# A linear-attention recurrence: products of k and v written into the SBUF state buffer and scanned there, two channel chunks per instruction

## The chip, the cores and the metric

The kernel runs on one core of a Trainium2 chip. A core has five engines that run their own instruction streams and meet at semaphores: TensorE (PE, matrix products into PSUM; PEld in the profile is its loading of weights), VectorE (DVE), ScalarE (ACT), GpSimd (POOL) and SyncE (SP, which issues DMAs). SBUF and PSUM are the two on-chip memories, both with 128 partitions. The metric is the device time of one execution in microseconds, median of the runs. All data are fp32.

## What is computed

Sixteen sequences of 256 tokens by 512 channels pass through an encoder-decoder block (self attention, cross attention, MLP) and then an RWKV-like block. The change is in the recurrence of the second block. Cut to what matters, with H = 32 heads of S = 16 channels:

```
w = exp(-exp(time_decay + tanh(xw @ decay_w1) @ decay_w2)).reshape(B, L, H, S)
r, k, v = ((x_ @ W_.T).reshape(B, L, H, S) for x_, W_ in (...))
s0 = state[:, i0 + 2:i0 + 2 + S].reshape(B, H, S, S)

def step(s, inp):
    k_l, v_l, w_l, r_l = inp
    a = k_l[..., :, None] * v_l[..., None, :]
    out = jnp.einsum('bhs,bhst->bht', r_l, faaaa * a + s)
    return (a + w_l[..., None] * s, out)
_, outs = jax.lax.scan(step, s0, seq)        # over the 256 tokens
```

So for each channel (head, s) and each of the 16 value columns t of its head there is a first-order recurrence over the tokens: state(l+1) = w(l) state(l) + k(l) v(l). The output reads the state before it is updated, times r, summed over s. A group norm, a gate, an output product and a channel-mixing part follow.

## The kernel before

The program has four phases, one after the other: self attention (tiles s_), cross attention (x_), MLP (b_), and phase_c with the second block (c_). Only phase_c is touched. It starts about 2420 us into the span and takes the last 1830.

**Layout.** Channels lie on partitions: 512 channels are 4 chunks (KC = 4) of 128, tokens (T = 256) run along the free dimension. A tile is 128 x 4 x 256. `pair(x, i)` is chunks 2i and 2i+1, thus 128x512.

**Stages.** `phase_c` is a software pipeline written out by hand: `body(k, parts, par)` works, in one iteration, on the recurrence of sequence k ("wkv"), on what follows it for sequence k - 1 ("back": group norm, gate, Wo, channel mixing) and on what comes before it for sequence k + 1 and k + 2 ("front", "norm"). 14 iterations (k = 1 to 14) hold both wkv and back; k = 0 has no back, k = 15 no front. Each iteration has RS = 16 steps n, one for each value column. The table FILLS says which PSUM units (mw0, k0, o0, ...) TensorE fills at step n ahead of and behind the second half step; VectorE or ScalarE empties them. Each engine runs the same loop over n in its own order, so that table is the order of all four.

**The recurrence.** At step n:

- PE, `broadcast_v` (L1645): for each half step i = 0, 1, one matmul spreads column n of v over the 16 channels of its head, into `vb` in PSUM, chunks 2i and 2i+1. It waits until VectorE is done with what step n - 1 left there.
- DVE, `recur` (L1474, L1479): multiplies vb by kT in place in PSUM, then runs one TENSOR_TENSOR_SCAN for each of the two chunks, from wT (SBUF) and vb (PSUM), starting at s0, into `S[:, n % 4, c, 1:257]` in SBUF. S has four buffers, one for each of four steps in turn.
- ACT, `start_state` (L1355): copies s0 into column 0 of the S buffer.
- POOL (L1201): after both half steps and the start state, multiplies all four chunks of S by rT in place (128x1024). Called z here.
- PE, `sum_states` (L1656): at odd steps, sums z of an earlier pair of steps over the channels of each head into `acc`. With this the S buffers are free again (semaphore summed).

**Other work of the same engines in an iteration.** VectorE reads PSUM units (L1423 for the five mixes mw, mk, mr, mv, mg; L1430 r; L1436 and L1437 v; L1445 o; L1453 kv; L1427 g), takes norm statistics (L1405 to L1412) and the group norm's (L1489, L1493 to L1502). GpSimd has, besides z, five adds of 128x1024 after the five mixes (`add_xa`, L1159), the group norm (L1164 to L1173), the gate product zT times g2T (L1181, step 3), the inverse deviation (L1152, L1154), the shifted difference and the two sums of the channel mixing (L1186 at step 8, L1191 at steps 9 and 10), and L1194, L1212, L1216 at steps 15, 12 and 13. Each stands in POOL's queue right behind z of its step. The two channel-mixing sums release TensorE's product with fWk (unit kk0, step 11).

## Time and profile before

| | |
|---|---|
| median of 3 runs | 4260.67 us (4258.37 to 4265.11) |
| the profiled execution | 4252.74 us, span 4250.9 us |
| busy in the span | PE 88%, DVE 71%, ACT 48%, POOL 41% |
| one iteration of phase_c with all parts | about 105.5 us |
| busy in one such iteration (us) | PE 98.7, DVE 84.4, POOL 65.1, ACT 32.9 |

The profile is one execution on the core, read by a hardware profiler. Busy time of PE is modelled and includes overlap of a matmul with the next one, so 98.7 of 105.5 us is an order that is almost gapless, not a peak rate. A time in brackets behind a row is how long the engine was idle before it, and what released it. What one iteration costs is set stretch by stretch by the engine that has no idle time there.

### The profile page before, as it was taken

The numbers are of one execution on the slowest core, as the hardware profiler recorded it, in microseconds if no ns is written. First come the engines' busy times: TensorE is split into PE (matmuls) and PEld (weight loads), VectorE is DVE, ScalarE is ACT, GpSimd is POOL, SyncE is SP. The second block draws the span as 40 slices with busy tenths as digits, with TensorE's granted clock in tenths as the row PEclk, the third lists the DMA queues.
The fourth block names the chain that finished last, engine by engine and source line by source line (L and its number), as shares of the span: only waits on it lengthen the run. The fifth ranks groups of instructions, "written<-read, shape, count | busy, mean of one in ns | idle before, by whom it ended". The sixth has DMA issues, their size and how long they took to land. (4 is left out here: it accounts for less than half of the span.)

```text
span 4250.9 us, 71399 instructions
## 1 busy us (share of the span) xinstructions
PE 3730.4 (88%) x21636; PEld 2882.3 (68%) x21636; DVE 2998.0 (71%) x6732; ACT 2057.8 (48%) x5384; POOL 1742.2 (41%) x1210
## 2 busy tenths in 40 slices
PE   5998998588888886999999778999999999999976
PEld 4777777477777774899999655666666666666643
DVE  5777777477777775556556338888888878888872
ACT  4777777367777675545545322333333333333322
POOL 2444444144444441000000135666666666666652
PEclk9999999799999997999999889999999999999988
DMA  3434434344444443010010210000000000000000
GB/s 110 104 99 109 104 99 104 96 116 118 104 114 110 122 104 116 30 44 30 30 41 33 73 50 18 24 24 23 24 23 24 23 24 23 24 23 23 23 18 15
DMA packets 146611, 256.58 MB, mean 60 GB/s; under 512 B 27184, under 2 KB 32048, under 8 KB 145424
## 3 DMA queue, kind: packets, MB, share of 16 engines
q1 hardware_dynamic: 146448, 254.49, 22.0%
q8 instruction: 92, 1.51, 0.2%
q14 instruction: 71, 0.58, 0.0%
HBM read 107.62 MB, written 33.55 MB: 33 GB/s over the span
## 5 line engine op out<-in xcount | busy, mean ns | idle before, releaser
L1201 POOL TENSOR_TENSOR c_S<-c_S,c_rT 128x1024 f32<-128x1024 f32 x256 | 558.1, 2180 | 458.4 <-DVE c_S L1479 417.6
L1479 DVE TENSOR_TENSOR_SCAN c_S<-c_wT,c_s,c_vb 128x256 f32<-128x256 f32 x1024 | 709.0, 734 | 45.0 <-issue 2.7
L1474 DVE TENSOR_TENSOR c_vb<-c_kT,c_vb 128x512 f32<-128x512 f32 x512 | 352.4, 688 | 286.4 <-PE c_vb L1645 255.6
L348 POOL TENSOR_TENSOR x_prob<-x_prob,x_rsums 128x512 f32<-128x512 f32 x256 | 275.2, 1075 | 477.7 <-DVE x_rsums L510 477.7
L348 POOL TENSOR_TENSOR s_prob<-s_prob,s_rsums 128x512 f32<-128x512 f32 x256 | 275.2, 1075 | 431.0 <-DVE s_rsums L510 431.0
L1645 PE MATMUL c_vb<-c_vhl,c_spread 128*128 128x512 f32 x512 | 300.4, 597 | 73.6 <-DVE c_S L1479 60.6
L404 ACT ACTIVATE x_prob<-x_t,x_tmin 128x256 f32<-128x256 f32 x512 | 256.4, 502 | 218.3 <-DVE x_tmin L503 218.0
L404 ACT ACTIVATE s_prob<-s_t,s_tmin 128x256 f32<-128x256 f32 x512 | 256.5, 502 | 193.9 <-DVE s_tmin L503 193.6
L862 PE MATMUL b_ps<-b_ln_high,b_w_high 128*128 128x256 f32 x1024 | 290.9, 284 | 14.8 <-DVE b_ln_low L804 14.8
L863 PE MATMUL b_ps<-b_ln_low,b_w_high 128*128 128x256 f32 x1024 | 290.8, 284 | 0.0
L864 PE MATMUL b_ps<-b_ln_high,b_w_low 128*128 128x256 f32 x1024 | 290.8, 284 | 0.0
L499 DVE SCALAR_TENSOR_TENSOR x_ps_s<-x_ps_s,x_mask 128x512 f32<-128x512 f32 x256 | 177.8, 695 | 93.7 <-PE x_ps_s L592 72.9
L499 DVE SCALAR_TENSOR_TENSOR s_ps_s<-s_ps_s,s_mask 128x512 f32<-128x512 f32 x256 | 177.6, 694 | 90.3 <-PE s_ps_s L592 62.7
L1159 POOL TENSOR_TENSOR c_xmix<-c_xmix,c_xaT 128x1024 f32<-128x1024 f32 x80 | 174.1, 2176 | 145.8 <-DVE c_xmix L1423 135.1
L602 PE MATMUL x_ps_t<-w_ident,x_prob 128*128 128x128 f32 x1024 | 163.3, 283 | 71.8 <-ACT x_probT L414 62.6
L760 ACT ACTIVATE b_shared<-b_ps,w_cols 128x256 f32<-128x256 f32 x256 | 123.3, 481 | 206.8 <-PE b_ps L864 204.9
L503 DVE CUSTOM_DVE_ANT_0 x_t<-x_ps_s,x_mneg 128x256 f32<-128x256 f32 x512 | 197.1, 422 | 31.0 <-issue 3.3
L503 DVE CUSTOM_DVE_ANT_0 s_t<-s_ps_s,s_mneg 128x256 f32<-128x256 f32 x512 | 197.1, 422 | 29.3
L602 PE MATMUL s_ps_t<-w_ident,s_prob 128*128 128x128 f32 x1024 | 161.8, 281 | 59.7 <-ACT s_probT L414 51.0
L862 PEld LDWEIGHTS b_ps<-b_ln_high,b_w_high 128*128 128x128 f32 x1024 | 197.7, 193 | 15.8 <-ACT b_ln_high L748 15.2
L862 PE MATMUL b_ps<-b_w_high,b_act_high 128*128 128x512 f32 x512 | 201.6, 394 | 5.1 <-DVE b_act_low L825 5.0
L863 PE MATMUL b_ps<-b_w_low,b_act_high 128*128 128x512 f32 x512 | 199.5, 390 | 0.0
(266 smaller groups left out, 10572.4 us busy)
## 6 DMA issues: line engine op xcount, KB each, us to landing
s_stack<-s_parts_qk SPq DMA_DIRECT2D x384, 128.0 KB, 2.4
x_stack<-x_parts_qk SPq DMA_DIRECT2D x384, 128.0 KB, 2.4
s_x_in<-in_x SPq DMA_DIRECT2D x16, 512.0 KB, 3.6
s_xb<-in_x SPq DMA_DIRECT2D x16, 512.0 KB, 4.1
x<-s_x_out SPq DMA_DIRECT2D x16, 512.0 KB, 4.8
x_enc<-in_ctx SPq DMA_DIRECT2D x16, 512.0 KB, 4.4
x_x_in<-x SPq DMA_DIRECT2D x16, 512.0 KB, 3.7
x_xb<-x SPq DMA_DIRECT2D x16, 512.0 KB, 4.1
```

Source lines behind the costliest of these rows:

```text
L348: nc.gpsimd.tensor_tensor(prob[:, h % 4, :, :], prob[:, h % 4, :, :], rsums[:, h, :].unsqueeze(2).to_broadcast([P, TC, T]), ALU.mult).then ...
L404: op = nc.scalar.activation(prob[:, n % 4, tc, :], t[:, n % 2, tc, :], ACT.Exp, bias=tmin[:, n, tc:tc + 1], scale=-1.0, accum_out=psums[:, ...
L499: nc.vector.scalar_tensor_tensor(ps_s[:, n % 2, :, :], ps_s[:, n % 2, :, :], -SCALE, mask[:, :, :], ALU.mult, ALU.mult)
L503: op = nc.vector.tensor_tensor_reduce(out=t[:, n % 2, tc, :], in0=ps_s[:, n % 2, tc, :], in1=mneg[:, tc, :], scale=1.0, scalar=3.0e38, op0 ...
L602: op = nc.tensor.transpose(ps_t[:, h % 2, kc, tc * P:(tc + 1) * P], prob[:, h % 4, tc, kc * P:(kc + 1) * P], w["ident"][:, :])
L862: nc.tensor.matmul(out, sh, mh, start=start, stop=False)
L863: nc.tensor.matmul(out, sh, ml, start=False, stop=False)
L864: return nc.tensor.matmul(out, sl, mh, start=False, stop=stop)
L1201: nc.gpsimd.tensor_tensor(S[:, n % 4, :, 0:T], S[:, n % 4, :, 0:T], rT[:, par, :, :], ALU.mult).then_inc(z_ready, 1)
L1474: nc.vector.tensor_tensor(pair(vb, i), pair(kT[:, par, :, :], i), pair(vb, i), ALU.mult)
L1479: op = nc.vector.tensor_tensor_scan(S[:, n % 4, c, 1:T + 1], wT[:, par, c, :], vb[:, c, :], s0[:, par, c, n:n + 1], ALU.mult, ALU.add)
L1645: nc.tensor.matmul(pair(vb, i), spread[:, place, :], pair(vhl[:, par, slab, :, :], i), start=True, stop=True).then_inc(vb_filled, 1)
```

## The change

`S` loses its extra column (T + 1 becomes T). `recur` no longer works in PSUM: the product of kT and vb for tokens 0 to 254 goes to columns 1 to 255 of the S buffer in SBUF, for both chunks of the half step, and one scan over 512 columns runs on S in place, from wT and S. Column 0 of each chunk holds s0, put there by ScalarE; the decay tile wT is shifted by one token and has a 0 in column 0 of each chunk, so the scan starts afresh at the second chunk. The wait of TensorE's `broadcast_v` is now on the product (vb_read), no longer on the scan; the waits for a free S buffer (summed) and for the start state (a0_ready) are now VectorE's, ahead of the product and ahead of the scan; GpSimd's wait for the start state is gone. `start_state` moves to the head of each step in ScalarE's order. v is spread in half steps as before.

```diff
-        S = sb("S", P, 4, KC, T + 1)
+        S = sb("S", P, 4, KC, T)
...
+                nc.gpsimd.memset(wT[:, :, :, 0], 0.0)
...
                         if "wkv" in parts:
-                            pool.wait_ge(a0_ready, step(k, n))
                             pool.wait_ge(scanned, half(k, n, 1))
-                            nc.gpsimd.tensor_tensor(S[:, n % 4, :, 0:T], S[:, n % 4, :, 0:T], rT[:, par, :, :],
+                            nc.gpsimd.tensor_tensor(S[:, n % 4, :, :], S[:, n % 4, :, :], rT[:, par, :, :],
...
-                            op = nc.scalar.activation(wT[:, other, 2 * i + c, :], channels(name)[:, c, :], ACT.Exp,
+                            op = nc.scalar.activation(wT[:, other, 2 * i + c, 1:T], channels(name)[:, c, 0:T - 1], ACT.Exp,
...
                     for n in range(RS):
+                        if "wkv" in parts:
+                            start_state(k, n, par)
                         if n > 0:
                             take(k, FILLS[n - 1][1], parts, par)
...
-                        if "wkv" in parts:
-                            start_state(k, n, par)
                         take(k, FILLS[n][0], parts, par)
...
                     if n == 0 and i == 0:
-                        dve.wait_ge(s0_loaded, 16 * k + 16)
                         dve.wait_ge(w_ready, k + 1)
-                    dve.wait_ge(vb_filled, half(k, n, i))
-                    nc.vector.tensor_tensor(pair(vb, i), pair(kT[:, par, :, :], i), pair(vb, i), ALU.mult)
-                    nc.vector.drain()
                     if i == 0 and (not first(k) or n >= 4):
                         dve.wait_ge(summed, k * (RS // 2) + ((n - 4) // 2 + 1))
-                    for c in (2 * i, 2 * i + 1):
-                        op = nc.vector.tensor_tensor_scan(S[:, n % 4, c, 1:T + 1], wT[:, par, c, :], vb[:, c, :],
-                                                          s0[:, par, c, n:n + 1], ALU.mult, ALU.add)
-                    op.then_inc(scanned, 1)
+                    dve.wait_ge(vb_filled, half(k, n, i))
+                    s = S[:, n % 4, 2 * i:2 * i + 2, :]
+                    nc.vector.tensor_tensor(s[:, :, 1:T], pair(kT[:, par, :, 0:T - 1], i), pair(vb, i)[:, :, 0:T - 1],
+                                            ALU.mult).then_inc(vb_read, 1)
+                    nc.vector.drain()
+                    if i == 0:
+                        dve.wait_ge(a0_ready, step(k, n))
+                    nc.vector.tensor_tensor_scan(flat(s), flat(wT[:, par, 2 * i:2 * i + 2, :]), flat(s), 0.0, ALU.mult,
+                                                 ALU.add).then_inc(scanned, 1)
...
-                        pe.wait_ge(scanned, half(k, n - 1, i))
+                        pe.wait_ge(vb_read, half(k, n - 1, i))
...
-                                                  gather[:, 24 - 8 * o:56 - 8 * o], pair(S[:, n % 4, :, 0:T], i),
+                                                  gather[:, 24 - 8 * o:56 - 8 * o], pair(S[:, n % 4, :, :], i),
```

VectorE's queue at step 1 of a full iteration before the change (c_vb is the spread v in PSUM, c_S the state buffer, the scan shows as SCALAR_TENSOR_TENSOR; L1489 and L1423 belong to other work):

```order
L1474 TENSOR_TENSOR c_vb<-c_kT,c_vb 128x512 [waits c_vb_filled]
L1479 SCALAR_TENSOR_TENSOR c_S<-c_wT,c_s,c_vb 128x256 [waits c_summed]
L1479 SCALAR_TENSOR_TENSOR c_S<-c_wT,c_s,c_vb 128x256
L1489 TENSOR_TENSOR c_b<-c_acc,c_bonusT 128x1024 [waits c_summed]
L1421 ISA
L1423 TENSOR_TENSOR c_xmix<-c_ps,c_sx 128x512 [waits c_filled]
L1421 REGISTER_ALU
L1423 TENSOR_TENSOR c_xmix<-c_ps,c_sx 128x512 [waits c_filled]
```

The same place with the change (L1426 is what was L1423, and L1493 what was L1489):

```order
L1484 SCALAR_TENSOR_TENSOR c_S<-c_wT,c_S 128x512 [waits c_a0_ready]
L1493 TENSOR_TENSOR c_b<-c_acc,c_bonusT 128x1024 [waits c_summed]
L1424 ISA
L1426 TENSOR_TENSOR c_xmix<-c_ps,c_sx 128x512 [waits c_filled]
L1424 REGISTER_ALU
L1426 TENSOR_TENSOR c_xmix<-c_ps,c_sx 128x512 [waits c_filled]
L1477 REGISTER_ALU
L1479 TENSOR_TENSOR c_S<-c_kT,c_vb 128x2x255 [waits c_vb_filled]
L1484 SCALAR_TENSOR_TENSOR c_S<-c_wT,c_S 128x512
```

Two scans of 256 columns with one SBUF tensor and one PSUM tensor became one scan of 512 columns with both tensors in SBUF; the order of the other rows is kept.

GpSimd's queue around steps 3 and 4 before the change (z is L1201, the gate product L1181, an add after a mix L1159):

```order
L1200 REGISTER_ALU [waits c_a0_ready]
L1201 TENSOR_TENSOR c_S<-c_S,c_rT 128x4x256 [waits c_scanned]
L1180 REGISTER_ALU
L1181 TENSOR_TENSOR c_b<-c_b,c_g2T 128x1024 [waits c_emptied_act]
L1199 REGISTER_ALU
L1200 REGISTER_ALU [waits c_a0_ready]
L1201 TENSOR_TENSOR c_S<-c_S,c_rT 128x4x256 [waits c_scanned]
```

And with the change (z is now L1204, the gate product L1185):

```order
L1203 REGISTER_ALU
L1204 TENSOR_TENSOR c_S<-c_S,c_rT 128x1024 [waits c_scanned]
L1184 REGISTER_ALU
L1185 TENSOR_TENSOR c_b<-c_b,c_g2T 128x1024 [waits c_emptied_act]
L1203 REGISTER_ALU
L1204 TENSOR_TENSOR c_S<-c_S,c_rT 128x1024 [waits c_scanned]
```

GpSimd's order is the same; z lost a wait, and its S operand is one run of 1024 columns, no longer four runs of 256 with a gap of one between them.

## Rows read from the trace of the kernel before

**Rows 1.** The page: busy time, share of the span, instructions.

```profile
PE 3730.4 (88%) x21636; PEld 2882.3 (68%) x21636; DVE 2998.0 (71%) x6732; ACT 2057.8 (48%) x5384; POOL 1742.2 (41%) x1210
```

**Rows 2.** Windows: stretch, length, busy us (count) by engine, granted clock.

```profile
core 0: us, PE busy (x) PEld busy (x) DVE busy (x) ACT busy (x) POOL busy (x), PEclk, DMA share, GB/s
3000.00:3105.50 105.50, 98.70 (x423) 66.05 (x422) 84.37 (x134) 32.94 (x76) 65.14 (x37) 0.97 0.08 24
...
3111.00:3116.00 5.00, 4.35 (x19) 2.44 (x20) 4.55 (x7) 2.07 (x6) 2.18 (x1) 0.66 0.00 0
3116.00:3141.50 25.50, 25.50 (x88) 13.95 (x86) 15.41 (x23) 5.57 (x16) 12.87 (x6) 1.00 0.05 21
3141.50:3166.00 24.50, 21.49 (x113) 15.51 (x112) 23.18 (x36) 10.63 (x21) 17.36 (x12) 1.00 0.08 24
```

**Rows 3.** Groups of VectorE in one iteration: count, busy us, mean ns.

```profile
L1479 DVE TENSOR_TENSOR_SCAN c_S<-c_wT,c_s,c_vb 128x256 f32<-128x256 f32 x65 | 45.1, 734 | 3.0 <-issue 0.2
L1474 DVE TENSOR_TENSOR c_vb<-c_kT,c_vb 128x512 f32<-128x512 f32 x33 | 22.7, 689 | 17.6 <-PE c_vb L1645 16.8 <-issue 0.8
L1423 DVE TENSOR_TENSOR c_xmix<-c_ps,c_sx 128x512 f32<-128x512 f32 x10 | 6.3, 675 | 0.0
L1489 DVE TENSOR_TENSOR c_b<-c_acc,c_bonusT 128x1024 f32<-128x1024 f32 x1 | 1.2, 1198 | 0.0
```

**Rows 4.** Groups of GpSimd in the same iteration.

```profile
L1201 POOL TENSOR_TENSOR c_S<-c_S,c_rT 128x1024 f32<-128x1024 f32 x16 | 34.9, 2180 | 26.2 <-DVE c_S L1479 23.9 <-ACT c_S L1355 2.3
...
L1181 POOL TENSOR_TENSOR c_b<-c_b,c_g2T 128x1024 f32<-128x1024 f32 x1 | 2.4, 2359 | 1.1 <-ACT c_b L1267 1.1
```

**Rows 5.** Timeline of VectorE, steps 0 to 11: start, length.

```profile
3140.43 1.39 DVE L1479 TENSOR_TENSOR_SCAN c_S<-c_wT,c_s,c_vb 128x256 f32<-128x256 f32 x2
...
3159.86 1.38 DVE L1479 TENSOR_TENSOR_SCAN c_S<-c_wT,c_s,c_vb 128x256 f32<-128x256 f32 x2
3161.16 0.67 DVE L1474 TENSOR_TENSOR c_vb<-c_kT,c_vb 128x512 f32<-128x512 f32 x1
3161.98 1.39 DVE L1479 TENSOR_TENSOR_SCAN c_S<-c_wT,c_s,c_vb 128x256 f32<-128x256 f32 x2
3163.28 0.67 DVE L1474 TENSOR_TENSOR c_vb<-c_kT,c_vb 128x512 f32<-128x512 f32 x1
3164.03 1.39 DVE L1479 TENSOR_TENSOR_SCAN c_S<-c_wT,c_s,c_vb 128x256 f32<-128x256 f32 x2
...
3211.09 1.38 DVE L1479 TENSOR_TENSOR_SCAN c_S<-c_wT,c_s,c_vb 128x256 f32<-128x256 f32 x2
```

**Rows 6.** Timeline of GpSimd: group norm's first and last, channel mixing's first sum.

```profile
3157.73 0.29 POOL L1164 TENSOR_TENSOR c_gtmp<-c_grstd 128x64 f32<-128x64 f32 x1
...
3159.50 1.93 POOL L1173 TENSOR_TENSOR c_b<-c_b,c_grstd 128x1024 f32<-128x1024 f32 x1
...
3202.22 2.18 POOL L1191 TENSOR_TENSOR c_b<-c_b,c_xcT 128x1024 f32<-128x1024 f32 x1
```

**Rows 7.** Timeline of TensorE: the wait of step 13's broadcast, the first fWk product.

```profile
3111.65 0.50 PE L1645 MATMUL c_vb<-c_vhl,c_spread 128*128 128x512 f32 x1 [2.81 <-DVE c_S L1479]
...
3206.33 3.72 PE L1545 MATMUL c_ps<-c_b,c_fWk 128*128 128x256 f32 x16
```

**Rows 8.** Timeline in phase b: GpSimd and VectorE at one moment.

```profile
1684.58 2.61 POOL L715 TENSOR_TENSOR b_xb<-b_xb,b_row_b 128x1024 f32<-128x1024 f32 x1 [35.91 <-DMA b_x_in<-x]
...
1685.00 2.74 DVE L814 TENSOR_TENSOR b_shared<-b_shared 128x512 f32<-128x512 f32 x1
...
1688.15 0.69 DVE L814 TENSOR_TENSOR b_shared<-b_shared 128x512 f32<-128x512 f32 x1
```

**Rows 9.** Timeline in self attention: two VectorE subtractions, one GpSimd product, one elsewhere.

```profile
122.47 2.12 DVE L462 TENSOR_TENSOR s_ln_low<-s_lnT,s_ln_high 128x512 fp32r<-128x512 f32 x2
...
122.64 1.41 POOL L348 TENSOR_TENSOR s_prob<-s_prob,s_rsums 128x512 f32<-128x512 f32 x1 [3.23 <-DVE s_rsums L510]
...
149.66 1.04 POOL L348 TENSOR_TENSOR s_prob<-s_prob,s_rsums 128x512 f32<-128x512 f32 x1
```

**Rows 10.** Line 1479 over 1500 us: shortest, median, longest scan in ns.

```profile
L1479 DVE TENSOR_TENSOR_SCAN c_S<-c_wT,c_s,c_vb x916: 719/736/751, 2639.9 to 4139.5; 128x256 f32<-128x256 f32 x184
```

More of the change, by code:

```diff
@@ L1013, in phase_c @@
         th_ready, g_used = sem("th_ready"), sem("g_used")
-        a0_ready, w_ready, vb_filled, scanned = sem("a0_ready"), sem("w_ready"), sem("vb_filled"), sem("scanned")
+        a0_ready, w_ready, vb_filled, vb_read = sem("a0_ready"), sem("w_ready"), sem("vb_filled"), sem("vb_read")
+        scanned = sem("scanned")
         z_ready, summed, acc_read = sem("z_ready"), sem("summed"), sem("acc_read")
@@ L1305, in move @@
                             nc.scalar.drain()
-                            nc.scalar.activation(wT[:, other, :, :], wT[:, other, :, :], ACT.Exp, scale=-1.0).then_inc(w_ready, 1)
+                            nc.scalar.activation(wT[:, other, :, 1:T], wT[:, other, :, 1:T], ACT.Exp, scale=-1.0).then_inc(w_ready, 1)
                     elif what == "k":
```

## Prediction

> **What bounds the kernel now.** I read the page first, for the shares of the span: TensorE is busy for 88% [rows 1]. That mean hides what matters for a change in the recurrence, so the second view was the busy time by stretch. A full iteration of phase_c takes 105.5 us, with TensorE busy for 98.7, VectorE for 84.4 and GpSimd for 65.1 [rows 2]. It falls in two kinds of stretch. From 3116 to 3141.5 TensorE has no idle time and VectorE is busy for 15.4 of 25.5 us. From 3141.5 to 3166 it is the other way round: VectorE is busy for 23.2 of 24.5 us and TensorE waits for it [rows 2]. The recurrence's steps 1 to 11 run mostly in stretches of the second kind, so there each microsecond that VectorE gains or loses counts, until TensorE's product with fWk begins [rows 7], from where TensorE sets the pace to the end of the iteration.
>
> In a bare step (step 4) VectorE starts a product at 3161.16 and the next at 3163.28: 2.1 us for a half step, of which the two scans are 1.39, or 0.73 for the first and 0.65 more for the second [rows 3, 5]. GpSimd is idle for 26.2 us of the iteration waiting for scans before z [rows 4], so z (2.18 us, 16 times) hides behind VectorE's next half steps.
>
> **Where the operands lie.** The old scan reads one tensor from SBUF (wT) and one from PSUM (vb). All its 916 durations lie between 719 and 751 ns [rows 10], although GpSimd works at its side for 62% of an iteration [rows 2]: such a scan and GpSimd do not disturb each other. The new scan reads wT and S, both in SBUF. The trace has no such scan, but it has other VectorE instructions with two SBUF tensors, and they do not run beside GpSimd. L814 takes 0.69 us alone; issued at 1685.00, while GpSimd's add ran from 1684.58 to 1687.19, it took 2.74 us and ended at 1687.74, 0.55 after GpSimd [rows 8]. In self attention two such subtractions take 2.12 us together, and the GpSimd product that starts in the first of them takes 1.41 instead of 1.04 us [rows 9]: the one that comes second stands until the first is through, in both directions. The Trainium skill's page "SBUF — State Buffer", section "Who interferes with whom", puts it as a rule that speaks against this change: a VectorE instruction with two SBUF inputs takes the read port that it shares with GpSimd, for its whole length. By that rule the trace agrees for products; a scan would be no exception, which no row here shows. By the rule the time is the sum below; with an undisturbed scan, as [rows 10] alone would have it, it is rival 1's.
>
> **What each part costs.**
> - Two scans become one. Its length is bounded by 1.38 us (the two of today) and by 1.0 (the 0.73 of one, and 0.26 for 256 more columns at the rate of L1489 against L1423: 1.198 less 0.675 for 512 [rows 3]). A scan's column is dearer than a product's, since one of 256 columns takes longer than a product of 512, so it is near the upper end: with a product's fixed part of 0.15 (0.675 less 0.525) the scan has 0.58 for 256 columns and 1.32 for 512; I take 1.27, between this and the second scan's 0.65. If it has stood before GpSimd its fixed part is partly over (0.55 for 0.69 in [rows 8]), so 1.12 us after GpSimd's end. Undisturbed, a half step would go from 2.08 to about 1.93.
> - The product goes to SBUF with one SBUF input: like L1423, 0.67 for 0.69, nothing.
> - z: S is now one run of 1024 columns. L1181, with both operands in one run, takes 2.36 against z's 2.18 [rows 4]. I take 2.36; the lower end is 2.18.
> - TensorE's broadcast is released by the product, 1.3 us earlier. Where VectorE is the bound this gives nothing; at step 13 TensorE's idle 2.81 us [rows 7] ends 1.4 us sooner.
> - The start state is now waited for by VectorE, behind which the scan, all its reads and so GpSimd and TensorE queue. ScalarE is busy for 33 of 105 us and makes the copy at the head of the step, behind reads that VectorE's own earlier ones wait for as well; nothing. If that cover failed at every step, a copy late by 0.2 us would cost 3 us an iteration. The wait for a free buffer moves ahead of a product that is 0.7 long, and the buffer was summed two steps before: nothing. The shifted decay and the memset: nothing, no path waits for one column less.
>
> **The sum.** Count a step from the end of one second scan to the end of the next. With the port held by one of the two engines, a step is: z with its start, 2.44 (VectorE's reads and the next product, up to 1.4 + 0.7, lie beside it); the first scan, 1.12; a gap; the second scan, 1.12. That is 4.68 and the gap. The gap is VectorE's reads and product, or the GpSimd instruction that stands behind z, whichever is longer: 2.05 for a waiting one of 2.18 (0.13 less, as L348 in [rows 9]: the first subtraction ends at about 123.14, 0.67 after its start, L348 0.91 later, for 1.04 alone); where GpSimd must first wait for mixes that are read in this very gap, the reads and 2.2. Before, the step lengths follow from VectorE's timeline (first and last of 12 scan ends, 3141.82 and 3212.47 [rows 5]; group norm from 3157.73 to 3161.43 [rows 6]):
>
> | step | before | gap, by what | after |
> |---|---|---|---|
> | 1 | 7.0 | 4.5: L1489 and mw reads 2.3, then the add | 9.2 |
> | 2 | 6.7 | 2.9: waiting add, then VectorE's small scalar op and product | 7.6 |
> | 3 | 5.7 | 3.6: group norm | 8.3 |
> | 4 | 4.2 | 2.2: gate product | 6.9 |
> | 5 | 8.2 | 2.0: waiting add | 6.7 |
> | 6 | 6.7 | 3.4: mv reads, then the add | 8.1 |
> | 7 | 7.4 | 3.0: o read and statistics, inverse deviation | 7.7 |
> | 8 | 6.3 | 3.4: mg reads, then the add | 8.1 |
> | 9 | 6.0 | 1.8: shifted difference | 6.5 |
> | 10 | 5.7 | 2.0: first mixing sum | 6.7 |
> | 11 | 6.8 | 2.0: second mixing sum | 6.7 |
>
> 70.7 us become 82.5, so 11.8 more. Step 5 gets shorter since it held 3.9 us of waiting for TensorE. The mixing sum now ends at 3204.40 [rows 6] plus 11.8, and TensorE, which began fWk 1.9 after it at 3206.33 [rows 7], has that slack; at step 13 the earlier broadcast gives 1.4. I take 10.4 us an iteration. 14 full iterations give 146; k = 0, with the five adds but no back, 6, and k = 15, with back but no adds, 10 by the same steps. 162 in all: 4252.7 of the profiled execution becomes 4415. The median of the runs shown stands 7.9 above it, so **4423 us**, 3.8% slower.
>
> **The rivals.**
> 1. *The scan does not take the port* (its two tensors come at a lower rate than a product's, and the rows show only products). Then each half step is 0.15 shorter, 3.3 over steps 1 to 11, TensorE's idle at step 13 ends 1.4 sooner, and the stretch after it, at a granted clock of 0.66 [rows 2], may stay at full clock, 1.7: 5 to 6.4 an iteration, 75 to 95 in all: 4175 us. It decides as soon as scans start while z runs. Chance 0.09. This is the side that the change looks good from: fewer and cheaper VectorE instructions.
> 2. *GpSimd goes first at each handover*: its next instruction, waiting behind z, gets the port before the scan that stands there. At the six steps where it waits already (2, 4, 5, 9, 10, 11) the first scan is 2.2 later and the second finds the port free: 0.9 more each, 5.7, of which the earlier mixing sum gives back some 1.5. 14 to 15 an iteration, 4480 us. L348 in [rows 9] got the port before a subtraction issued after it, which is order of arrival and speaks for the sum above; nothing in the trace shows two waiting. A granted clock that falls in TensorE's longer waits (to 1.2 GHz for part of 3111 to 3116, mean 0.66, after 2.81 us idle [rows 2, 7]) would add as much. Chance of either 0.17.
> 3. *The contention is real but mostly absorbed*: VectorE's 17.6 us idle before products [rows 3] swallow it, or z stays at 2.18 and the adds fall into reads. 1 to 5 an iteration: 4280 to 4330 us. Against it: the idle lies where TensorE sets the pace. Chance 0.08, and 0.04 for no change at all (4261).
>
> The sum's own case, 4335 to 4460, has 0.62.
>
> **Range and chances.** 4310 to 4510. Slower by over 0.2% (about what a measurement of this kernel can tell from no change): 0.87; within 0.2%: 0.04; faster: 0.09. z at 2.18 takes 2 us an iteration (28 in all), the scan at 1.0 a further 6, and with it the upper half of rival 3 is held from 4310 on; rival 2 leads to 4510. Left out are rival 1, no change, half of rival 3 and a tail above: 0.2.
>
> **What the profile after would show.** Scans of 512 columns in two classes: about 1.27 us, and up to 2.3 us longer, ending some 1.1 after the end of a GpSimd instruction; z and the adds with a longest value above 3 us where they came second; VectorE busy for over 100 us of an iteration of about 116; TensorE's waits before products that follow GpSimd (L1531, L1552, kk0) longer; the broadcast's waits for scans gone. If scans have one length with z at their side, the prediction is wrong in its main step, and the time comes out near rival 1. If they wait but TensorE's idle time does not grow, rival 3.

## The result and the profile after

The median is **4437.57 us** (4430.59 to 4452.31, 4 runs) against 4259.76 for the kernel before on the same chip (4258.37 to 4265.11, 4 runs): ratio 1.042, 95% interval 1.0392 to 1.0447. Slower by 178 us.

The page of the profiled execution: the span, the busy times (those of before in [rows 1]), and from its fifth part the costliest groups of phase_c.

```profile
span 4428.8 us, 70863 instructions
...
PE 3818.4 (86%) x21636; PEld 2932.4 (66%) x21636; DVE 3274.0 (74%) x6220; ACT 2059.5 (47%) x5384; POOL 1919.7 (43%) x1211
...
L1484 DVE TENSOR_TENSOR_SCAN c_S<-c_wT,c_S 128x512 f32<-128x512 f32 x512 | 988.9, 1931 | 60.7 <-issue 29.6
L1204 POOL TENSOR_TENSOR c_S<-c_S,c_rT 128x1024 f32<-128x1024 f32 x256 | 604.8, 2362 | 465.9 <-DVE c_S L1484 464.6
...
L1479 DVE TENSOR_TENSOR c_S<-c_kT,c_vb 128x510 f32<-128x510 f32 x512 | 343.3, 671 | 179.6 <-PE c_vb L1649 139.6
...
L1163 POOL TENSOR_TENSOR c_xmix<-c_xmix,c_xaT 128x1024 f32<-128x1024 f32 x80 | 201.6, 2521 | 159.9 <-DVE c_xmix L1426 147.9
```

VectorE has 512 instructions fewer and is busy 276 us longer. A scan of 512 columns takes 1.93 us in the mean, where two of 256 took 1.39 [rows 5].

The view of one line gives the shortest, the median and the longest duration in ns. Here are the scan, z, and GpSimd's add after a mix:

```profile
L1484 DVE TENSOR_TENSOR_SCAN c_S<-c_wT,c_S x512: 1224/1861/3383, 2508.6 to 4349.4; 128x512 f32<-128x512 f32 x171
```
```profile
L1204 POOL TENSOR_TENSOR c_S<-c_S,c_rT x256: 2342/2358/3278, 2513.5 to 4350.7; 128x1024 f32<-128x1024 f32 x128
```
```profile
L1163 POOL TENSOR_TENSOR c_xmix<-c_xmix,c_xaT x80: 2167/2180/3115, 2436.1 to 4202.6; 128x1024 f32<-128x1024 f32 x80
```

The old scans were all between 719 and 751 ns [rows 10]. The new one is 1224 ns at its shortest and up to 2.2 us longer. z takes 2.36 where it is alone; an add that took 2.17 to 2.18 alone reaches 3.1.

How the two engines alternate is seen in the timeline of VectorE and GpSimd at steps 3 and 4 (start, length, engine, line):

```profile
3111.66 0.65 DVE L1479 TENSOR_TENSOR c_S<-c_kT,c_vb 128x510 f32<-128x510 f32 x1
3111.81 2.35 POOL L1204 TENSOR_TENSOR c_S<-c_S,c_rT 128x1024 f32<-128x1024 f32 x1 [1.16 <-DVE c_S L1484]
...
3112.47 2.78 DVE L1484 TENSOR_TENSOR_SCAN c_S<-c_wT,c_S 128x512 f32<-128x512 f32 x1 [0.16 <-issue]
3114.13 3.26 POOL L1185 TENSOR_TENSOR c_b<-c_b,c_g2T 128x1024 f32<-128x1024 f32 x1
3115.17 0.65 DVE L1479 TENSOR_TENSOR c_S<-c_kT,c_vb 128x510 f32<-128x510 f32 x1
3115.92 2.55 DVE L1484 TENSOR_TENSOR_SCAN c_S<-c_wT,c_S 128x512 f32<-128x512 f32 x1
```

z runs from 3111.81 to 3114.16. The scan is issued at 3112.47, stands, and ends at 3115.25, 1.09 us after z. The gate product (L1185), issued at 3114.13, comes after that scan: 3.26 us, to 3117.39. The second scan, issued at 3115.92, ends at 3118.47, 1.08 after it. The product in between (L1479, one SBUF input) takes its usual 0.65 beside the running GpSimd instruction. I counted all scans above 1.5 us: 305 of 512. Each was issued while a GpSimd instruction ran, and each ends 1.076 to 1.089 us after that one.

The windows (stretch, length, busy us and counts by engine, granted clock, as in [rows 2]) show a full iteration, and the stretches where TensorE sets the pace:

```profile
2990.00:3108.00 118.00, 105.22 (x420) 70.09 (x421) 98.09 (x101) 32.97 (x76) 75.22 (x36) 0.90 0.07 21
3099.50:3168.90 69.40, 63.96 (x271) 45.66 (x270) 62.84 (x64) 20.66 (x48) 48.52 (x24) 0.90 0.07 20
...
3175.00:3180.00 5.00, 4.97 (x13) 3.33 (x14) 4.75 (x5) 2.12 (x6) 3.92 (x2) 0.50 0.02 5
3180.00:3205.00 25.00, 25.00 (x88) 13.74 (x91) 15.89 (x16) 4.29 (x12) 12.09 (x6) 0.98 0.06 21
```

An iteration takes 117.5 us (mean of the first 13 intervals between group norms' first reductions) for 105.5. VectorE is busy for 98.1 us and TensorE for 105.2, 6.5 more than before with the same matmuls. Its granted clock is 0.90 over the iteration, 0.97 before [rows 2]. All of the stretch from 3180 to 3205, like that from 3116 before, is gapless.

### The profile page after: what moved, and what is told of

Its sections match the earlier page's. It is cut to its first block and busy times, and to the rows that moved or that the text cites. A ratio compares the mean times of both kernels' runs of the same rounds, so it can differ in the third digit from the quotient of the medians.

```text
span 4428.8 us, 70863 instructions
## 1 busy us (share of the span) xinstructions
PE 3818.4 (86%) x21636; PEld 2932.4 (66%) x21636; DVE 3274.0 (74%) x6220; ACT 2059.5 (47%) x5384; POOL 1919.7 (43%) x1211
## 5 line engine op out<-in xcount | busy, mean ns | idle before, releaser
L1484 DVE TENSOR_TENSOR_SCAN c_S<-c_wT,c_S 128x512 f32<-128x512 f32 x512 | 988.9, 1931 | 60.7 <-issue 29.6
L1204 POOL TENSOR_TENSOR c_S<-c_S,c_rT 128x1024 f32<-128x1024 f32 x256 | 604.8, 2362 | 465.9 <-DVE c_S L1484 464.6
L1479 DVE TENSOR_TENSOR c_S<-c_kT,c_vb 128x510 f32<-128x510 f32 x512 | 343.3, 671 | 179.6 <-PE c_vb L1649 139.6
L1649 PE MATMUL c_vb<-c_vhl,c_spread 128*128 128x512 f32 x512 | 311.6, 619 | 65.7 <-DVE c_S L1479 43.3
L1163 POOL TENSOR_TENSOR c_xmix<-c_xmix,c_xaT 128x1024 f32<-128x1024 f32 x80 | 201.6, 2521 | 159.9 <-DVE c_xmix L1426 147.9
```

The source lines that it names most:

```text
L1204: nc.gpsimd.tensor_tensor(S[:, n % 4, :, :], S[:, n % 4, :, :], rT[:, par, :, :], ALU.mult).then_inc(z_ready, 1)
L1479: nc.vector.tensor_tensor(s[:, :, 1:T], pair(kT[:, par, :, 0:T - 1], i), pair(vb, i)[:, :, 0:T - 1], ALU.mult).then_inc(vb_read, 1)
L1484: nc.vector.tensor_tensor_scan(flat(s), flat(wT[:, par, 2 * i:2 * i + 2, :]), flat(s), 0.0, ALU.mult, ALU.add).then_inc(scanned, 1)
L1649: nc.tensor.matmul(pair(vb, i), spread[:, place, :], pair(vhl[:, par, slab, :, :], i), start=True, stop=True).then_inc(vb_filled, 1)
```

## The experiments

The kernel before ran beside each, and ratios go by those: 4257.09 us (21 runs) for the product in PSUM, the two scans, the dense state buffer and all moved waits together; 4260.49 (13) for the two runs without adds, z in halves and the full function in PSUM; 4255.47 (21) for the wait for a free buffer alone, the start state first alone and the late release; 4256.82 (12) for the start state waited for by VectorE.

### The scan of 512 columns, with the product in PSUM

The changed kernel, but the product stays in PSUM, and the broadcast waits for the scan. Left out: the shift by one token and the start state in the scan.

```diff
-                    nc.vector.tensor_tensor(s[:, :, 1:T], pair(kT[:, par, :, 0:T - 1], i), pair(vb, i)[:, :, 0:T - 1],
-                                            ALU.mult).then_inc(vb_read, 1)
+                    nc.vector.tensor_tensor(pair(vb, i), pair(kT[:, par, :, :], i), pair(vb, i), ALU.mult)
...
-                    nc.vector.tensor_tensor_scan(flat(s), flat(wT[:, par, 2 * i:2 * i + 2, :]), flat(s), 0.0, ALU.mult,
+                    nc.vector.tensor_tensor_scan(flat(s), flat(wT[:, par, 2 * i:2 * i + 2, :]), flat(pair(vb, i)), 0.0,
```

> The changed kernel with one edit: the product stays in PSUM (vb, in place, all 256 tokens) and the single scan of 512 columns reads wT from SBUF and vb from PSUM; the broadcast waits for the scan again. Left out: the shift by one token and the start state in the scan, so the numbers computed differ, not the work. All moved waits and the dense S stay. Port theory: the scan has one length, about 1.27 us, no GpSimd instruction gets longer than 2.4, half steps of 1.93 us, time 4190 to 4240. Rival, the moved waits or the merged scan's own length are the cause: the time stays above 4380.

Measured: **4238.48 us** (10 runs), ratio 0.9956 (0.9941 to 0.9970). Its scan and its z by line:

```profile
L1483 DVE TENSOR_TENSOR_SCAN c_S<-c_wT,c_vb x512: 1219/1221/1223, 2509.1 to 4152.3; 128x512 f32<-128x512 f32 x171
```
```profile
L1204 POOL TENSOR_TENSOR c_S<-c_S,c_rT x256: 2343/2357/2385, 2514.0 to 4153.6; 128x1024 f32<-128x1024 f32 x128
```

With one operand in PSUM no scan is lengthened (1.219 to 1.223 us) and no z either. Where the product and its scan lie is thus worth 4437.6 - 4238.5 = 199 us, more than the whole slowdown (196 when each is taken against the kernel before at its side: 178 above it and 18.6 below). The later release of the broadcast, which this run also has, is tested by itself below and changes nothing.

### Two scans of 256 columns, with the product in SBUF

The other half: the changed kernel with two scans for each half step, and S with its extra column, so that z has the four runs of before.

```diff
-        S = sb("S", P, 4, KC, T)
+        S = sb("S", P, 4, KC, T + 1)
...
-                    nc.vector.tensor_tensor_scan(flat(s), flat(wT[:, par, 2 * i:2 * i + 2, :]), flat(s), 0.0, ALU.mult,
-                                                 ALU.add).then_inc(scanned, 1)
+                    for c in (0, 1):
+                        op = nc.vector.tensor_tensor_scan(s[:, c, :], wT[:, par, 2 * i + c, :], s[:, c, :], 0.0, ALU.mult,
+                                                          ALU.add)
+                    op.then_inc(scanned, 1)
```

> The changed kernel with S in rows of 257 as before (z at 2.18 us) and two scans of 256 columns for each half step, both in SBUF in place: against the kernel before, only where the operands lie and the waits. Port theory: scans of 0.7 alone and of up to 3 us beside GpSimd, GpSimd may take the port between the two scans, time 4420 to 4520. Rival, a single in-place scan over 512 columns is itself the cost: within 20 us of 4260.

Measured: **4488.3 us** (4 runs), ratio 1.0547 (1.0529 to 1.0566). The scan by line:

```profile
L1485 DVE TENSOR_TENSOR_SCAN c_S<-c_wT,c_S x1024: 658/692/2783, 2515.5 to 4405.1; 128x256 f32<-128x256 f32 x171
```

The short scans stand as well: 359 of the 1024 take over 0.9 us, and each of them ends 0.544 to 0.556 us after the GpSimd instruction that ran when it was issued. The merged scan is not what costs: the changed kernel is 51 us faster than this one, although its z takes 2.36 us and z here 2.18.

### GpSimd's adds taken out, with the change and without

If the time is lost to the port, it must depend on what GpSimd has to do. GpSimd's five adds of 1024 columns after the mixes become adds of 2 columns, in both kernels; left out is that part of the sums.

```diff
-                    nc.gpsimd.tensor_tensor(xj, xj, xaT[:, :, 1:T + 1], ALU.add).then_inc(xj_ready, 1)
+                    nc.gpsimd.tensor_tensor(xj[:, 0, 0:2], xj[:, 0, 0:2], xaT[:, 0, 1:3], ALU.add).then_inc(xj_ready, 1)
```

With the change:

> The changed kernel with GpSimd's five adds after the mixes (128x1024 each, one iteration) cut to two columns; the output lacks these sums, all semaphores stay. Port theory: the gaps of steps 1, 2, 5, 6 and 8 shrink by about 2.2, 0.8, 1.3, 2.2 and 2.2 us, less what TensorE then sets, so 5 to 8 us an iteration and 75 to 120 us in all: 4320 to 4365. Rival, the lost time does not come from GpSimd instructions that stand between the scans: above 4410.

Without:

> The kernel before with the same five adds cut to two columns. Port theory: VectorE does not meet GpSimd here, only short waits of TensorE for an add go away: 4235 to 4260. Rival, the adds are on the path for another reason and would give the same gain in both kernels: below 4180.

Measured: **4357.4 us** with the change (4 runs, ratio 1.0230, 1.0213 to 1.0247), **4257.08 us** without (10 runs, 0.9991, 0.9981 to 1.0000). The same 80 adds of 2.2 us are worth 80 us in the changed kernel and nothing in the kernel before. So GpSimd's work has come onto the path of the changed kernel. That it came there by the port is shown by the run with the product in PSUM, whose GpSimd does the same work beside scans of one length.

### z in two halves

GpSimd multiplies each half step's 512 columns as soon as its scan is through, so that half of z can run in the gap between the scans.

```diff
-                            pool.wait_ge(scanned, half(k, n, 1))
-                            nc.gpsimd.tensor_tensor(S[:, n % 4, :, :], S[:, n % 4, :, :], rT[:, par, :, :],
-                                                    ALU.mult).then_inc(z_ready, 1)
+                            for i in range(2):
+                                pool.wait_ge(scanned, half(k, n, i))
+                                op = nc.gpsimd.tensor_tensor(pair(S[:, n % 4, :, :], i), pair(S[:, n % 4, :, :], i),
+                                                             pair(rT[:, par, :, :], i), ALU.mult)
+                            op.then_inc(z_ready, 1)
```

> The changed kernel with z in two instructions of 512 columns, each behind its own half step's scan, so each hold of the port is half as long and falls beside a product. Port theory: the wait of the first scan for z shrinks by about 1.1 us, the second scan now waits for a half z where its gap was short (steps 3, 4, 5, 9, 10, 11 have another GpSimd instruction there, which adds up instead): 0 to 4 us less an iteration, 4380 to 4440. Rival, order of issue and not the port: no change or, with 16 more GpSimd instructions an iteration, slower than 4450.

Measured: **4401.27 us** (4 runs), ratio 1.0329 (1.0312 to 1.0347). z by line:

```profile
L1205 POOL TENSOR_TENSOR c_S<-c_S,c_rT x512: 1256/1275/2282, 2521.7 to 4324.9; 128x512 f32<-128x512 f32 x171
```

36 us come back, although GpSimd has 0.19 us a step more to do (twice 1.275 for 2.36). It matters when GpSimd's work is issued, not only how much there is.

### The dense state buffer alone

The kernel before with S of 256 columns, no gap. The start state goes to a tile that nobody reads, and the shift by a token is left out.

```diff
-        S = sb("S", P, 4, KC, T + 1)
+        S, unused = sb("S", P, 4, KC, T), sb("unused", P, 4, KC)
...
-                        op = nc.vector.tensor_tensor_scan(S[:, n % 4, c, 1:T + 1], wT[:, par, c, :], vb[:, c, :],
+                        op = nc.vector.tensor_tensor_scan(S[:, n % 4, c, :], wT[:, par, c, :], vb[:, c, :],
```

> The kernel before with S in one run of 1024 columns; the scans write columns 0 to 255, ScalarE's copy of the start state goes to an unused tile (so the output lacks the shift by one token, the work is the same). Port theory with z's price from L1181: z goes from 2.18 to 2.36 us, which is hidden here, time 4255 to 4275. Rival, z's length is what costs: above 4300.

Measured: **4266.7 us** (10 runs), ratio 1.0023 (1.0012 to 1.0034). z is 2.36 instead of 2.18, for 256 times 0.18 = 46 us of GpSimd, of which about 10 reach the end: GpSimd is not the bound when the scans don't need its port.

```profile
L1201 POOL TENSOR_TENSOR c_S<-c_S,c_rT x256: 2339/2358/2382, 2513.3 to 4180.4; 128x1024 f32<-128x1024 f32 x128
```

### The moved waits alone

The kernel before, with the start state's copy at the head of ScalarE's step, VectorE and not GpSimd waiting for it, and VectorE's wait for a free buffer ahead of the product.

```diff
+                        if "wkv" in parts:
+                            start_state(k, n, par)
...
+                    if i == 0 and (not first(k) or n >= 4):
+                        dve.wait_ge(summed, k * (RS // 2) + ((n - 4) // 2 + 1))
                     dve.wait_ge(vb_filled, half(k, n, i))
...
-                    if i == 0 and (not first(k) or n >= 4):
-                        dve.wait_ge(summed, k * (RS // 2) + ((n - 4) // 2 + 1))
+                    if i == 0:
+                        dve.wait_ge(a0_ready, step(k, n))
```

> The kernel before with only the waits of the change: start_state at the head of the step, VectorE waits for the free buffer ahead of the product and for the start state ahead of the scans, GpSimd no longer. Port theory: no change, 4250 to 4270. Rival, the moved waits are the cause: most of the 177 us, above 4380.

Measured: **4272.76 us** (6 runs), ratio 1.0036 (1.0020 to 1.0051): above the range that I had given. I had priced these waits at nothing. Three more runs took them apart.

The wait for a free buffer ahead of the product, alone:

```diff
+                    if i == 0 and (not first(k) or n >= 4):
+                        dve.wait_ge(summed, k * (RS // 2) + ((n - 4) // 2 + 1))
                     dve.wait_ge(vb_filled, half(k, n, i))
```

> The kernel before with VectorE's wait for a free S buffer ahead of the product, and nothing else. It tells apart which of the moved waits costs the 12 to 15 us that the run with all of them moved (4272.8) showed. Theory A, ScalarE's place: in that run ScalarE stood at the head of steps for a free buffer for 51.4 us over 1500 us of the trace, 13.6 before, and its reads of PSUM behind that wait came later. Then this wait alone costs nothing: 4256 to 4264 us. Rival B, VectorE's wait ahead of the product holds the product back: 4266 to 4276 us here.

The start state's copy first in ScalarE's step, alone:

```diff
                     for n in range(RS):
+                        if "wkv" in parts:
+                            start_state(k, n, par)
```

> The kernel before with the start state's copy at the head of each step in ScalarE's order, and GpSimd, not VectorE, waiting for it as before. Theory A (ScalarE's place costs the time of the moved waits): 4266 to 4278 us, and ScalarE's waits for summed buffers near 50 us over 1500. Rival B (VectorE's waits cost it): 4256 to 4264 us.

The same, with VectorE waiting for it and not GpSimd:

```diff
-                            pool.wait_ge(a0_ready, step(k, n))
...
+                    if i == 0:
+                        dve.wait_ge(a0_ready, step(k, n))
                     for c in (2 * i, 2 * i + 1):
```

> The kernel before with the start state's copy at the head of ScalarE's step and VectorE, not GpSimd, waiting for it ahead of the first scan; VectorE's wait for a free buffer stays where it was. The two other parts of the moved waits cost nothing alone (1.0002 and 0.9999), all together 1.0036. Theory A, the wait for the start state is what costs, since on VectorE it holds back the scan, all reads behind it and so TensorE: 1.003 to 1.005, 4268 to 4276 us. Rival B, only the combination with the wait for a free buffer ahead of the product costs: within 0.2%, 4248 to 4264 us.

Measured: **4257.55 us** (11 runs, 1.0002, 0.9993 to 1.0011); **4257.26** (11 runs, 0.9999, 0.9990 to 1.0008); **4270.4** (7 runs, 1.0037, 1.0024 to 1.0051). So the first two cost nothing, and my suspicion of ScalarE's place (it does stand longer there, 65.1 for 13.6 us over 1500) was wrong. With VectorE waiting for the start state the kernel takes 14 us more. VectorE's waits over 1500 us, and its timeline at one step (engine, line and what it waited for: us in total, times, longest):

```profile
DVE c_S L1480 <- issue: 28.5, 147, 0.5
...
DVE c_S L1480 <- ACT c_S L1354: 5.6, 24, 0.2
```
```profile
3165.49 0.69 DVE L1473 TENSOR_TENSOR c_vb<-c_kT,c_vb 128x512 f32<-128x512 f32 x1
3166.42 1.39 DVE L1480 TENSOR_TENSOR_SCAN c_S<-c_wT,c_s,c_vb 128x256 f32<-128x256 f32 x2 [0.23 <-issue]
```

It is hardly ever a late copy (24 times, 5.6 us). The gap between the product and the first scan of a step is longer, but not by one price for each wait. In the kernel before one wait (summed) stands there at every step from step 4 of k = 0 on. In the sequences whose code is written out with constants (k = 0, 13, 14 and 15) the gap is 0.07 to 0.08 us all the same, but for one late case. In the twelve that run in a loop it is 0.15 at the even steps but step 2, where VectorE's sequencer first computes the value to wait for (a register instruction of L1477 that starts 0.08 us ahead of the scan), and 0.07 to 0.08 at the others, where no such instruction stands between the two. With the start state's wait beside it the gap is 0.14 in the written-out sequences and mostly 0.16 or 0.23 in the loop. So a wait that is satisfied already added nothing by itself; a value that had to be computed, or a second wait, added 0.07 to 0.09. The mean gap over the same 1500 us went from 0.088 to 0.130; 0.042 times 512 half steps is 21 us, an upper end for the 14.

These gaps are not all of it. In the 13 iterations that I averaged, 13 us longer together, seven steps (1, 2, 3, 6, 8, 10 and 12) are 0.08 to 0.10 us longer each, but about half of the time, 6.4 us, lies in step 9 of four iterations, which takes 7.4 to 7.6 us there and 5.95 in the others (and in all 14 of the kernel before). TensorE has no idle time in that step; the granted clock, 1.00 otherwise, is down for a part of it. Two windows of this run, step 9 of k = 1 and of k = 5:

```profile
2663.50:2671.10 7.60, 7.60 (x32) 6.02 (x29) 4.06 (x8) 2.50 (x7) 4.20 (x3) 0.85 0.00 1
3092.40:3098.40 6.00, 6.00 (x28) 5.26 (x29) 4.10 (x8) 2.58 (x7) 4.21 (x3) 1.00 0.00 1
```

With all waits moved, where the mean gap is only 0.103, step 9 is long in eight iterations, 12.4 us in all, which is most of what that run costs. With the start state first it was long once, with the wait for a free buffer alone never. These are counts of one execution each, and why small delays bring the lower clock to this step is not shown.

The changed kernel has the start state's wait at each step as well, with a mean gap of 0.125 over the same 1500 us and this row:

```profile
DVE c_S L1484 <- issue: 29.0, 177, 0.2
```

### The earlier release of the broadcast undone

The changed kernel with TensorE waiting for the scan.

```diff
-                        pe.wait_ge(vb_read, half(k, n - 1, i))
+                        pe.wait_ge(scanned, half(k, n - 1, i))
```

> The changed kernel with TensorE's broadcast waiting for the scan again, no longer for the product: one part of the change undone, to price the earlier release, for which I had taken 1.4 us an iteration off the sum (20 us in all). Theory A, it does give that at step 13, where TensorE still waits: 4452 to 4465 us. Theory B, the changed kernel's steps 1 to 11 have VectorE and GpSimd as bound and the release gives nothing there nor at step 13: 4432 to 4442 us. Theory C, the late release also delays products of VectorE in the gaps behind a long scan, of up to 3.4 us: 4470 to 4520 us.

Measured: **4434.83 us** (4 runs), ratio 1.0421 (1.0402 to 1.0440), no different from the changed kernel's 1.042. That is theory B's range, but not by its reason: the wait that I had in mind does change. TensorE at step 13 and behind it, first with the late release, then in the changed kernel:

```profile
3177.97 0.79 PE L1649 MATMUL c_vb<-c_vhl,c_spread 128*128 128x512 f32 x1 [3.38 <-DVE c_S L1484]
...
3180.56 1.35 PE L1535 MATMUL c_ps<-w_ident,c_xmix 128*128 128x128 f32 x8
...
3181.97 3.60 PE L1556 MATMUL c_ps<-c_fWr,c_b 128*128 128x512 f32 x8
```
```profile
3172.10 0.50 PE L1649 MATMUL c_vb<-c_vhl,c_spread 128*128 128x512 f32 x1 [2.00 <-DVE c_S L1479]
...
3175.03 1.97 PE L1535 MATMUL c_ps<-w_ident,c_xmix 128*128 128x128 f32 x8 [1.44 <-ACT c_xmix L1262]
...
3177.22 5.54 PE L1556 MATMUL c_ps<-c_fWr,c_b 128*128 128x512 f32 x8
```

The wait is 3.38 against 2.00: 1.38 us, as predicted (3.3 against 2.0 in the mean of 14 iterations). But the broadcast's successor (L1535) needs ScalarE's normalised xmix, which comes no sooner, so TensorE now waits 1.44 us there, and then the block with fWr takes 5.54 instead of 3.60 us: the clock in 3175 to 3180 is 0.50, the lower level. Why xmix is late is in GpSimd's row ahead of it, a tiny instruction of two columns that took 0.20 before:

```profile
3172.39 1.04 POOL L1158 TENSOR_TENSOR c_ln_shift<-c_ln_shift,c_ln_rstd 128x2 f32<-128x2 f32 x1
```

The scan from 3172.21 to 3173.44 holds it. With the late release this instruction takes just as long, but TensorE is still held at its broadcast when xmix comes, and needs no second wait. So the 1.38 us turns into another wait, and the clock falls behind it: from step 11 to the next step 0 it is at the lower level for 6.8 us in each of the 13 iterations of the changed kernel, for 3.4 us in 10 of them with the late release and in 12 of them in the kernel before. In that part TensorE is idle for 3.4 us in both kernels; its own work takes 32.8 us with the early release and 31.9 with the late one. The profiled iteration is thus even 0.7 us shorter with the late release (116.8 for 117.5), while the times of the whole program don't differ.

### The full function with the product in PSUM

To see whether the one scan can be had without the port: v is stored one element later, so TensorE spreads it shifted by one token, ScalarE writes the start state into column 0 of vb behind each broadcast, and the scan reads wT and vb. Nothing is left out.

```diff
-                    nc.scalar.copy(S[:, n % 4, :, 0], s0[:, par, :, n]).then_inc(a0_ready, 1)
+                    act.wait_ge(vb_filled, half(k, n, i))
+                    nc.scalar.copy(pair(vb, i)[:, :, 0], s0[:, par, 2 * i:2 * i + 2, n]).then_inc(a0_ready, 1)
...
+                    s, v = S[:, n % 4, 2 * i:2 * i + 2, :], pair(vb, i)
+                    nc.vector.tensor_tensor(v[:, :, 1:T], pair(kT[:, par, :, 0:T - 1], i), v[:, :, 1:T], ALU.mult)
...
+                    nc.vector.tensor_tensor_scan(flat(s), flat(pair(wT[:, par, :, :], i)), flat(v), 0.0, ALU.mult,
+                                                 ALU.add).then_inc(scanned, 1)
```

> A full version of the PSUM form: product in PSUM, one scan of 512 columns from wT and vb into S; v is stored one element later so that TensorE spreads it shifted by one token, and ScalarE puts the start state into column 0 of each chunk of vb behind each broadcast, ahead of the product. Port theory: scans of one length near 1.3 us; it gives 15 to 25 us as in the run with the product in PSUM and pays for 32 small ScalarE copies that now stand between broadcast and product: 4230 to 4290. Rival, VectorE's wait for ScalarE's queue costs more than a microsecond in each DVE-bound step: above 4350.

Measured: **4282.74 us** (4 runs), ratio 1.0051 (1.0033 to 1.0068). Its waits over 1500 us:

```profile
DVE c_vb L1484 <- ACT c_vb L1361: 323.8, 212, 4.3
```

The scan is undisturbed here too (1.220 to 1.223 us), but ScalarE's copy now stands between the broadcast and the product, 32 times an iteration. It does not beat the kernel before; no version with the whole function did.

## Why the prediction was right

The forecast was 4423 us (4310 to 4510), slower with 0.87; measured 4437.6. By the steps:

- **The scan takes the port**: right, and shown by each experiment that separates it. PSUM in place of SBUF gives 199 us back, less GpSimd work gives 80 back in this kernel and none in the other. The profile after has the two classes that the prediction named. The Trainium skill's page "SBUF — State Buffer", section "Who interferes with whom", puts the rule for a VectorE instruction with two SBUF inputs and does not name the scan among its instances; it holds for the scan too (1.22 against up to 3.38 us).
- **Its length**: 1.27 taken, 1.224 measured; after GpSimd's end 1.12 taken, 1.08 measured. z: 2.36 taken and measured.
- **Who goes first at a handover** (rival 2): order of arrival, so the scan that stands goes ahead of the GpSimd instruction issued later. L1185 above is one of many. Rival 2's other half, the clock, came true in part: 0.97 to 0.90. It raised TensorE's busy time by 6.5 us an iteration, but the lengths of steps 1 to 11 (below) came out without it; behind step 13 it did cost time.
- **The table of steps 1 to 11**: predicted 9.2, 7.6, 8.3, 6.9, 6.7, 8.1, 7.7, 8.1, 6.5, 6.7, 6.7, sum 82.5. Read from the ends of second scans (3204.95 and 3214.12 for step 1, 3103.57 for step 2, then one by one to 3168.93 for step 11): 9.17, 7.45, 8.16, 6.74, 6.88, 8.02, 7.43, 8.04, 6.91, 6.60, 6.58, sum 81.98. None is off by more than 0.41. This is the longest kind of iteration; their sums run from 80.95 to 81.98, and in the mean of 13 it is 81.4, with no step off by more than 0.27. All but one of the means lie below the table.
- **The 1.4 us for the earlier release**: wrong, the term that was mis-sized. In the means of 13 iterations (each from the end of step 0 to the next one's) steps 1 to 11 go from 70.8 to 81.4 us, 10.6 more where the table had 11.8. The rest of the iteration goes from 34.7 to 36.1: 1.4 longer instead of 1.4 shorter. TensorE is idle there for 2.8 us before and 3.4 after (2.1 at the broadcast and 1.2 at L1535), and its work takes 32.8 us for 31.9, at a mean granted clock of 0.91 for 0.96. Undoing the release changed nothing: the wait did get 1.4 shorter, but I had not looked at what TensorE needs next, nor at GpSimd's small instructions, which now stand behind scans. Over 14 iterations this term is 2.8 times 14 = 39 us, and the steps that came out shorter take 17 off. In the first and last sequence 16 us were taken, and 178 less 14 times 12.0 = 10 measured. With the three the sum comes to 4439 for 4437.6. So part of the closeness of 4423 is luck: the release was too good and the table too dear.
- **What the profile after would show**: the two classes of scans, the long z and adds, and the broadcast's wait for scans gone came true. VectorE is busy for 98, not over 100 us. TensorE's waits in steps 1 to 11 grew from 4.4 to 9.1 us an iteration, but mostly before products that wait for VectorE's reads (L1608, L1602 and L1591, which were L1604, L1598 and L1587: from 1.7 to 2.7, from 0.1 to 1.6 and from 0.6 to 1.3); of those behind GpSimd that I had named, only L1535 (L1531 before) grew by more than 0.2, from 0.4 to 1.1.
- **Moved waits at nothing**: the wait for a free buffer and ScalarE's place did cost nothing. VectorE's wait for the start state cost 14 us in the kernel before, hardly by a late copy: by a longer gap ahead of the scans, and by the lower clock in step 9 of some iterations. In the changed kernel it was not measured by itself; where a scan stands before GpSimd anyway, a gap of 0.08 us can hide.
- **Rival 1's price** (4175, an undisturbed scan) was too good. With the scan undisturbed the run gave 4238, an iteration shorter by 0.8 us (104.7 for 105.5, means of 13) where I had worked out 5 to 6.4. Of the 63 us between the two figures the wait for the start state is 14 and the dense z 10, by their prices alone; in that run the broadcast was also released late. The rest was not taken apart.

As a ledger of the 178 us: product and scan in SBUF +196 (from 18.6 below to 178 above), the wait on VectorE about +14, the dense z about +10, and the merged scan, as what remains, about -42. The last is by difference alone; that the parts add up was not tested. The run with two scans in SBUF speaks against it: 53 us separate it from the changed kernel (231 and 178 above the kernel before), with z cheaper there, so that the merged scan would be worth about -63 by that pair.

## What to carry to other kernels

Before a VectorE instruction that is issued hundreds of times is moved from PSUM to SBUF, look at what GpSimd does at its side: with two SBUF inputs the two engines take turns, each as long as the other's whole instruction, and the sum can be worked out step by step from durations in the old trace. Where an early release shortens a wait, follow the waiting engine to its next instruction; if that one needs something that comes no sooner, nothing is won. Put no second wait, and none whose value is computed in the loop, between two dependent VectorE instructions of an inner loop if another engine with slack can take it.

## What the runs showed of the hardware

- A scan of 512 columns takes 1.221 us from SBUF and PSUM and 1.224 with both tensors in SBUF: where its operand lies does not change its own length. Two of 256 in PSUM take 1.39, in a row.
- A column of a scan costs 1.9 ns (1.221 less 0.736 over 256), a column of a product 1.02 ((1.198 less 0.675) over 512, [rows 3]). The Trainium skill's page "DVE: opcode table, instruction layouts, handler registers and perf-mode slots", section "Datapath and trigger behaviour", says that the scan runs at half throughput; these rows agree.
- GpSimd's product of 1024 columns takes 2.36 us with S in one run and 2.18 with S in four runs, 257 apart, with the same S and rT. Why the dense one is slower is not settled.
- VectorE's small TENSOR_SCALAR of 2 columns stands before GpSimd as well, in both kernels. L1411 before and L1414 after take 0.17 us where no z runs, and 0.70 to 0.77 and 0.87 to 0.89 where they are issued in the middle of one; its neighbour L1415, issued at the end of z, takes 0.16:

```profile
3108.70 0.70 DVE L1411 TENSOR_SCALAR c_ln_ve<-c_ln_mv 128x2 f32<-128x2 f32 x1
```
```profile
3170.50 0.89 DVE L1414 TENSOR_SCALAR c_ln_ve<-c_ln_mv 128x2 f32<-128x2 f32 x1
3171.30 0.16 DVE L1415 TENSOR_SCALAR c_ln_shift<-c_ln_mv 128x2 f32<-128x2 f32 x1
```

- One wait of VectorE that is satisfied already added nothing to the gap of 0.07 to 0.08 us between product and scan where its value was a constant. A value computed in the loop, or a second wait, added 0.07 to 0.09 each.
- The product that writes SBUF is followed by its scan 0.09 us later, the one that writes PSUM 0.075, in the second half step, where no wait stands between.
